# Fused audio tower on one core: the first guesses of four reciprocal square roots computed by ScalarE in place of VectorE

## What is computed

```python
h = einsum('bfh,kh->bfk', frames(x, 128), dct)          # 32 x 313 rows of 128
n = layernorm(h); h = h + softmax(n @ n.T) @ n           # attention inside a clip, eps 1e-5
q = (layernorm(h) @ Wq.T + bq).reshape(b, s, 8, 64)
q = (q - mean) / sqrt(var + 1e-5) * ln_g + ln_b
s0, s1 = l2norm(q[..., :32]) @ l2norm(keys0).T, l2norm(q[..., 32:]) @ l2norm(keys1).T
sc0, ix0 = top_k(s0, 16); sc1, ix1 = top_k(s1, 16)       # 64 scores each
fs, pos = top_k(sc0 + sc1, 16)                           # over the 16 x 16 sums
w = softmax(fs); fi = (ix0 + ix1) at pos
h = h + sum_k gelu(h . expert_down[fi]) * w * expert_up[fi]
```

## Time and profile before

| | |
|---|---|
| median of 3 runs | 2027.36 us (2024.80 to 2029.87) |
| profiled execution | 2031.43 us |
| its span | 2029.6 us, 47236 instructions |
| PE busy | 1632.5 us (80%) |
| DVE busy | 1919.0 us (95%) |
| ACT busy | 1232.0 us (61%) |
| POOL busy | 1433.2 us (71%) |
| mean granted PE clock | 0.812 of full speed |

### The profile page before, as it was taken

One profiled execution on the slowest core, in us unless ns is written; L12 is line 12 of the kernel. 1 busy time (PEld: TensorE's weight loads), 2 busy tenths in 40 slices (PEclk: granted clock), 3 DMA queues, 4 the chain that ended last, 5 costly groups with the idle time before them and its releaser, 6 DMA issues.

```text
span 2029.6 us, 47236 instructions
## 1 busy us (share of the span) xinstructions
PE 1632.5 (80%) x11023; PEld 1169.5 (58%) x11023; DVE 1919.0 (95%) x15718; ACT 1232.0 (61%) x3883; POOL 1433.2 (71%) x2561
## 2 busy tenths in 40 slices
PE   5577888788888888888888788888878888986667
PEld 3235566566656655665666556656656565655456
DVE  2499999999999999999999999999999999999992
ACT  3346666666666666566556766656675665665554
POOL 2247777686777767777776777777687777767775
PEclk8877888888888787888888787888888888788765
DMA  1000000000000000000000000000000000000000
GB/s 44 7 10 4 19 7 13 13 7 19 7 19 9 13 13 6 19 7 19 7 6 22 6 19 7 19 7 7 19 9 20 7 19 7 6 13 9 7 6 11
DMA packets 46669, 24.87 MB, mean 12 GB/s; under 512 B 4827, under 2 KB 46116, under 8 KB 46390
## 3 DMA queue, kind: packets, MB, share of 16 engines
q1 hardware_dynamic: 46390, 21.85, 3.9%
HBM read 11.58 MB, written 10.26 MB: 11 GB/s over the span
## 4 chain that ended last, share of the span: by engine, by line
DVE 79%; PE 11%; ACT 5%; issue 4%; POOL 1%; SPq 1%; DMA 0%; DVEq 0%; ACTq 0%
DVE idx L1071 11%; DVE idx L1078 11%; DVE hrest L1065 10%; DVE alpha L1039 10%; DVE vals L1069 7%; DVE vals L1062 7%; DVE c L1109 5%; DVE crest L1103 5%; DVE top L1106 3%; DVE top L1100 3%; PE QB L526 2%; DVE beta L1044 2%; PE FB L418 1%; PE QB L514 1%; DVE lo L1033 1%
## 5 line engine op out<-in xcount | busy, mean ns | idle before, releaser
L914 POOL TENSOR_TENSOR bw<-beta,wp 128x1024 bf16<-128x1024 bf16 x240 | 505.2, 2135 | 347.3 <-issue 171.6
L526 PE MATMUL QB<-bw,alpha 128*128 128x48 bf16 x5120 | 554.5, 277 | 106.7 <-issue 101.1
L526 PEld LDWEIGHTS QB<-bw,alpha 128*128 128x128 bf16 x5120 | 521.0, 150 | 149.2 <-issue 139.4
L749 ACT ACTIVATE WD<-QB 32x96 f32<-32x96 f32 x1280 | 307.6, 240 | 84.5 <-PE QB L526 71.6
L1039 DVE TENSOR_SCALAR alpha<-hi 128x1024 bf16<-128x1024 bf16 x640 | 274.9, 502 | 0.0
L475 PE MATMUL SC<-WK,hidT 128*128 128x512 f32 x320 | 241.0, 846 | 12.6 <-issue 11.8
L1071 DVE FIND_INDEX8 idx<-vals,sraw 128x8 uint32<-128x64 f32 x1280 | 250.6, 218 | 0.0
L1078 DVE FIND_INDEX8 idx<-vals,hrest 128x8 uint32<-128x64 f32 x1280 | 250.6, 219 | 0.0
L1065 DVE MATCH_REPLACE8 hrest<-vals,sraw 128x64 f32<-128x64 f32 x1280 | 249.6, 207 | 0.0
L1062 DVE MAX8 vals<-sraw 128x8 f32<-128x64 f32 x1280 | 169.1, 207 | 14.1 <-ACT sraw L729 14.1
L1069 DVE MAX8 vals<-hrest 128x8 f32<-128x64 f32 x1280 | 166.6, 208 | 0.0
(11 more groups left out here) (206 smaller groups left out, 3583.3 us busy)
## 6 DMA issues: line engine op xcount, KB each, us to landing
res<-h_scratch SPq DMA_DIRECT2D x80, 64.0 KB, 1.9
xin<-in_x SPq DMA_DIRECT2D x32, 128.0 KB
h_scratch<-h2n SPq DMA_DIRECT2D x32, 128.0 KB
out<-ofin SPq DMA_DIRECT2D x64, 64.0 KB, 1.5
h_scratch<-h2n SPq DMA_DIRECT2D x32, 28.5 KB
out<-ofin SPq DMA_DIRECT2D x16, 57.0 KB
xin<-in_x SPq DMA_DIRECT2D x32, 28.0 KB
xin<-in_x SPq DMA_DIRECT2D x32, 0.2 KB
```

The source lines that it names most:

```text
L526: last = mm(bank[:, 48 * u:48 * u + 48], alpha[:, buf, a, :, 8 * p + u], bwv[:, :, a, :, 8 * p + u], start=(a == 0), stop=(a == 1))
L749: last = A(WD[r, RING[(t - 4) % NT], :, 8 * p:8 * p + 8], blocks[r, :, :, g], ACT.Copy)
L914: last = tt(bw[:, buf, NY * i:NY * i + NY, :], beta[:, buf, :, :], wp[:, buf, i, :].unsqueeze(1).to_broadcast([128, NY, 256]), ALU.mult)
```

## The change

The first guesses, the minus halves and the row means of the places (1) to (4) are computed by ACT. The guess for the keys stays with DVE. On ACT the mean is an `Identity` with a scale and a bias tile, minus half a `Copy` with a scale, the guess an `Identity` with integer input and output and a bias tile. For (1) ACT now takes the sums of squares of both clips first, then mean and guess, then the copies `hcs`. For (3) ACT waits for `v3`, for (4) for the last result of `norms`, at slot (0, 3). POOL waits for `stat_full` ahead of `half_norms`, and sets the two constants at the start. The diff:

```diff
+        cseed = sb("cseed", [128, 2])
...
+            def guess(x_, xh, y, done):
+                A(xh, x_, ACT.Copy, scale=-0.5)
+                A(y.bitcast(I32), x_.bitcast(I32), ACT.Identity, scale=-0.5, bias=cseed[0:x_.shape[0], 0:1]).then_inc(done, 1)
+            def row_guess(i, j):
+                part, mean = (s["ss1_full"], s["sv1"]) if i == 0 else (s["ss2_full"], s["sv2"])
+                act.wait_ge(part, 2 * j + 2)
+                A(sv[i][:], ss[i][:], ACT.Identity, scale=1.0 / D, bias=cseed[:, 1:2]).then_inc(mean, 1)
+                act.wait_ge(mean, j + 1)
+                guess(sv[i][:], sxh[i][:], sy[i][:], s["seed1_full"] if i == 0 else s["seed2_full"])
...
                         squares(ss[0], lambda c, n: bank[0:n, 129 * c:129 * c + D], xns, b, s["ss1_full"])
+                    row_guess(0, j)
+                    for b in range(2):
+                        bank = f_wait(act, f"hc{b}", j)
                         after(act, s["h2c_full"], 2 * j + b - 1)
...
                         squares(ss[1], lambda c, n: h2c[0:n, b, c, :], hid, b, s["ss2_full"])
+                    row_guess(1, j)
...
+                if (t, p) == (3, 3):
+                    act.wait_ge(s["v3_full"], j + 1)
+                    guess(v3[:], xh3[:], y3[:], s["seed3_full"])
...
+                if p == 3 and t == 0 and exists(k, 0, 0):
+                    act.wait_ge(s["n2_steps"], 2 * k + 2)
+                    guess(n2[:], xh4[:], y4[:], s["seed4_full"])
...
+                nc.gpsimd.memset(cseed[:, 0:1], RSQRT_MAGIC)
+                nc.gpsimd.memset(cseed[:, 1:2], 1e-5)
...
+                pool.wait_ge(s["stat_full"], j + 1)
...
-            def row_seed(i, j, done):
-                dve.wait_ge((s["ss1_full"], s["ss2_full"])[i], 2 * j + 2)
-                V.tensor_scalar(sv[i][:], ss[i][:], 1.0 / D, 1e-5, ALU.mult, ALU.add).then_inc((s["sv1"], s["sv2"])[i], 1)
-                dve.wait_ge((s["sv1"], s["sv2"])[i], j + 1)
-                seed(sv[i][:], sxh[i][:], sy[i][:], done)
...
-                if (t, p) == (0, 1) and j == 0:
-                    row_seed(0, j, s["seed1_full"])
...
-                if (t, p) == (2, 1):
-                    row_seed(1, j, s["seed2_full"])
...
-                    dve.wait_ge(s["v3_full"], j + 1)
-                    seed(v3[:], xh3[:], y3[:], s["seed3_full"])
...
-                dve.wait_ge(s["n2_steps"], 2 * j + 2)
-                seed(n2[:], xh4[:], y4[:], s["seed4_full"])
...
-                            if k + 1 < PAIRS:
-                                row_seed(0, k + 1, s["seed1_full"])
```

## The result

The kernel after takes 2030.61 us (median of 20 runs, 2028.81 to 2032.88), the kernel before 2025.94 us (20 runs beside them, 2022.61 to 2029.87): the ratio is 1.0021, 95% interval 1.0015 to 1.0027. It is 4.7 us slower, less than the 0.3% that was set as "no change", 10.6 us above the forecast and just outside the range. The profiled executions can't show this difference: the one of before, at 2031.43 us, was slower than all 20 timed ones, that of after (2030.61 us, span 2028.8) is an average one.

The account below looks back on a forecast made before the run. It took a cycle through DVE, ACT, PE and POOL as the bound: -0.6 + 0.74 - 0.7 = -0.56 us a regular pair, over eleven pairs plus 0.6 us 6.8 us, so 2027.4 - 7 = 2020 us; range 2004 to 2030.

Parts of the forecast that it names:

- The reading that ports bind DVE: DVE's 95% busy time includes waits for ports held by POOL, as at place (3); work moved to ACT escapes them.
- (c): Place (3): DVE loses 1.15 us a pair on average; ACT gets 0.35 us beside POOL's `bw`, nothing on the cycle.
- (a): Places (4) and (1), slot (0, 2): five instructions leave DVE's own leg of the cycle, gain 0.6 us a pair.
- the cycle as it was drawn: Each pair: DVE (slot 1), ACT and PE (slots 1 to 3), POOL (slot 4), DVE (`alpha`, `beta`, slot 0).
- (b): Place (2): ACT's mean, minus half and guess ahead of `h2n` cost 0.74 us on the cycle, bounds 0.3 and 1.0.
- (e): `alpha` in slot (4, 2): `beta` follows `Ye` at once, -1.8 us; POOL pushed more, +1.1; together -0.7 us a pair.
- two distances of 66.4 us: From ACT's wait for `c2` at slot 1 to POOL's `bw` at (3, 3): 66.42 and 66.35 us in two pairs.
- (d): Place (4) on ACT, 0.42 us at slot (0, 3): no wait, and POOL needs it only 10 us on.
- The cycle gives nothing back: Rival: comparisons push POOL by their full length, or ACT's addition is 1.0 us; 2027 to 2030 us, chance 0.28.
- DVE sets the pace alone: Rival: all DVE loses counts, 34 us, giving 1993 us, or about 2005 in half the pairs; chance 0.14 together.
- table load: Rival: integer `Identity` at (2, 1) makes ACT load tables ahead of the second guess, 36 us, 2056 us; chance 0.05.

Follow-up runs that it names:

- the slower kernel with less work: Places (1), (3) and (4) on ACT, (2) on DVE, and two Newton steps at place (3), against the kernel before: 2020.80 us, ratio 0.9971.
- the slowest: The kernel after with two more POOL additions to a scratch tile behind the Newton steps of place (3): 2075.61 us, 1.0228 against the kernel before.
- the one at 2003.88 us: The kernel after with two Newton steps instead of three at place (3): 2003.88 us, ratio 0.9876 against the kernel before.

## Why the prediction was wrong

**The reading that ports bind DVE** held. `bw` delays the guess of place (3); on ACT, with no other change, place (3) wins 0.38%, about 8 us of the 15 x 1.15 = 17 us that term (c) took from DVE. In the kernel after MAX8 begins 0.4 us behind `v3`, with two reads of PSUM between them:

```profile
872.48 0.18 DVE L1021 TENSOR_SCALAR v<-FB 128x40 f32<-128x40 f32 x1
...
872.88 2.11 DVE L1074 MAX8 vals<-sraw 128x8 f32<-128x64 f32 x16
```

**The failed step** is term (a), the gain of 0.6 us a pair in slot 0, and behind it the cycle as it was drawn, DVE -> ACT and PE -> POOL -> DVE, on which DVE's slot 0 lies in every pair. Part by part, for eleven pairs: (b) was to cost 8.1 us, and place (2) alone cost 9.3. (e) was to give 7.7, and place (3) alone gave 7.7. (a) was to give 6.6, and places (1) and (4) alone cost 2.6. That is 9 of the 11.7 us between the forecast and the result. In the trace of the kernel with (1) and (4) alone the chain does not use DVE's slot 0, and in the kernel after it does not use DVE at all: there is a second way from POOL to the next pair, `stdin` -> PE -> ACT, with no DVE in it, and it is as long. That DVE's saving in slot 0 counted at all was argued from two distances of 66.4 us, "the same, although DVE got there differently". These two pairs were not typical: over the 14 pairs of that trace the distance runs from 64.5 to 66.5 us.

With it failed the sentence in (a) that ACT's wait at `xns` "covers (b) to (d) together, with half a us left". The 3.2 us were a mean over pairs, in a state in which DVE still set the pace in part. Once DVE was quicker and ACT fuller, ACT waited there in three pairs only.

**(b)** was right in size: 0.73 us in the trace. That it has a price is shown three times, 9.3 us with place (2) alone, 10.7 us with the three instructions added to the kernel before, some 14 us back when it alone goes back to DVE. The nearness of 10.7 to 11.0 is partly luck, since one more instruction of 0.3 us at the same place made the kernel after faster. **(c)** and **(d)** cost nothing on ACT that shows.

**(e)**: `alpha` in slot (4, 2) stood at 5.4 to 5.5 us in ten pairs of before and 3.8 or 3.9 in four, and at 5.5 to 5.6 in most pairs of after, where 6 or more were named. `beta` began 1.04 us before the end of `Ye`, not with it. With place (3) alone on ACT there is even another form of it. In three of its pairs POOL is shut out, as here:

```profile
643.65 0.91 POOL L922 TENSOR_TENSOR wz<-wexp,rz 128x432 f32<-128x432 f32 x1
...
644.47 2.77 DVE L1058 TENSOR_SCALAR alpha<-hi 128x1024 bf16<-128x1024 bf16 x8
...
644.64 4.33 POOL L927 TENSOR_TENSOR Yw<-wz,m 128x432 f32<-128x432 f32 x1
...
647.15 0.63 DVE L1063 TENSOR_SCALAR beta<-lo 128x256 bf16<-128x256 bf16 x4
```

The sum of the two engines' delays in slot 4 was thus right in kind only. Its value for the pair depends on which of them the next pair waits for, and the term assumed DVE. That its -7.7 us equals the gain of place (3) is therefore no proof of it: the guess of place (3) also stands ahead of POOL's Newton steps, on the chain of the kernel with (1) and (4) alone.

**The rivals.** "The cycle gives nothing back" (2027 to 2030 us, chance 0.28) is what happened, down to the sign that it named: DVE waits for `zexp` at slot 3 in most pairs. Its reasons, pushes of a full comparison or 1.0 us on ACT, did not: ACT's addition measured 0.73 us, and it lies on a lap without DVE. "DVE sets the pace alone" is refuted by the run that gives DVE its instructions back for 5.5 us. No table load was added.

**The range** missed by 0.6 us. What it lacked is a term for the pace itself. Steps of 0.2 to 0.7 us a pair gave from -21 to +45 us by the medians where sums give 3 to 10. A sum over pairs had no claim to be good to a few microseconds, and a forecast of -7 us here was below what such a sum can tell.

## What to carry to other kernels

Before work is moved off the busiest engine, draw every way by which one iteration's end reaches the next one's start, and look for one that doesn't pass that engine: if it is nearly as long, the moved work must not go to an engine on it. A kernel may have two such ways of nearly equal length, and then work taken from one of them gives little. Here the engine with 62% of busy time was the wrong place for 0.73 us, and leaving that one part behind (all but place (2) on ACT) turned 0.2% slower into 0.5% faster. In a kernel whose iterations repeat to hundredths of a microsecond, judge a small edit by timed runs with its neighbours (a little more, a little less work), not by one number.

## What the runs showed of the hardware beyond that

Two engines that need the same ports have two ways to share them. In the earlier trace rows and in slot (4, 2) of the kernel after, DVE's `alpha` and POOL's instructions took turns: eight comparisons stretched to 5.4 to 5.6 us, `Yw` and `Ye` lost a few tenths. In the pair with place (3) alone on ACT that is shown above, `alpha` began 0.09 us before the end of `wz` and ran its eight comparisons in 2.77 us, as if alone, while `Yw` took 4.33 us, where 1.3 to 1.5 is usual: `beta` was over at 647.78, and `Yw` 1.19 us later, about what one such instruction takes. Twelve instructions of DVE kept POOL out, although each of them is 0.16 to 0.35 us long. It happened five times in the traces of that kernel and of the one with all but place (2) on ACT, three times to `Yw` and twice to `wz` (4.1 us in place of 0.9 to 1.1). The Trainium skill, "SBUF — State Buffer", section "SBUF: two separate sides", says that whoever starts first has the ports for the whole instruction; the turns agree with that, the stream does not follow from it. What decides between them was not tested and stays open. In all five `alpha` began within 0.1 us of a POOL instruction's start or end, but so it did in other pairs in which the two took turns.

The granted clock of TensorE is part of a steady kernel's state. Averaged over a profile it hardly tells the kernels apart (0.81 for after, 0.787 for the slower kernel with less work, 0.78 for the slowest, 0.822 for the one at 2003.88 us); in the 16 us behind the handover from POOL it is 0.73 for after and 0.50 for the next two, and in the last one it takes turns between 0.70 and 0.82 while its pairs take turns between 118.9 and 116.7 us.
